# Attention scores and a graph layer's product as sums of three products of split fp32 operands

## The reference

```python
def _sparse_attention(x, src, dst, wq, bq, wk, bk, wv, bv, wo, bo):
    q = (x @ wq + bq).reshape(N, H, Dh) * Dh ** (-0.5)
    k = (x @ wk + bk).reshape(N, H, Dh)
    v = (x @ wv + bv).reshape(N, H, Dh)
    scores = jnp.einsum('ehd,ehd->eh', q[src], k[dst])
    ...
    out = jax.ops.segment_sum(attn[:, :, None] * v[dst], src, num_segments=N)
    return out.reshape(N, D) @ wo + bo
for i in range(NUM_BLOCKS):
    y = _cond_layer_norm(x, cond, s1_w[i], s1_b[i], b1_w[i], b1_b[i])
    x = x + _sparse_attention(y, src, dst, wq[i], ...)
    y = _cond_layer_norm(x, cond, s2_w[i], s2_b[i], b2_w[i], b2_b[i])
    x = x + jax.nn.relu(y @ m_w1[i] + m_b1[i]) @ m_w2[i] + m_b2[i]
...
out = jnp.zeros_like(x).at[col].add(x[row] * norm[:, None])
return out @ lin_w.T + lin_b
```

## Time and profile before

| | us |
|---|---|
| runs before, median of 3 (lowest to highest) | 1582.38 (1581.98 to 1583.31) |
| the profiled execution, its own time | 1580.26 |
| span of its profile | 1578.6 |
| TensorE busy | 1504.3 |
| VectorE busy | 1186.9 |
| ScalarE busy | 1076.5 |
| mean granted clock of TensorE | 0.99 |

### The profile page before, as it was taken

How to read it: one execution, slowest core, us unless ns; L and a number is a source line. 1 busy time by engine, 2 the same in 40 slices (tenths; PEclk the granted TensorE clock), 3 DMA queues, 4 the chain that set the end, 5 groups by cost and what they waited for, 6 DMA issues and landing times. The chain is left out here.

```text
span 1578.6 us, 26154 instructions
## 1 busy us (share of the span) xinstructions
PE 1504.3 (95%) x9086; PEld 1212.8 (77%) x9086; DVE 1186.9 (75%) x2055; ACT 1076.5 (68%) x1557; POOL 644.8 (41%) x468
## 2 busy tenths in 40 slices
PE   4999899999999999999999999999999999999987
PEld 4775687888788878887864688888888888888874
DVE  8998565656565656564733499999999999999967
ACT  8845455544564546454532389999999999999953
POOL 3541200120012001200301677888888888888501
PEclk9999899999999999999999999999999999999989
DMA  3002310122012201110204877777777777777600
GB/s 111 1 1 89 127 54 28 34 64 79 26 34 81 76 12 34 61 61 27 96 0 160 183 168 150 155 157 153 156 155 153 157 151 158 152 157 153 156 34 34
DMA packets 88590, 151.48 MB, mean 96 GB/s; under 512 B 23610, under 2 KB 28602, under 8 KB 88002
## 3 DMA queue, kind: packets, MB, share of 16 engines
q0 software_dynamic: 54400, 85.33, 27.7%
q1 hardware_dynamic: 34114, 65.15, 12.6%
HBM read 141.02 MB, written 9.31 MB: 95 GB/s over the span
## 5 line engine op out<-in xcount | busy, mean ns | idle before, releaser
L1911 POOL DMA_INDIRECT edge_gathered<-dst_table,edge_index x158 | 271.2, 1716 | 58.1 <-issue 36.9
L227 PE MATMUL edge_z2p<-edge_w_hi,edge_h_hi 128*128 128x512 f32 x628 | 252.2, 402 | 0.6 <-DVE edge_late L2278 0.6
L227 PE MATMUL edge_z2p<-edge_w_lo,edge_h_hi 128*128 128x512 f32 x628 | 248.0, 395 | 0.0
L1090 POOL TENSOR_TENSOR h<-h,tr_row_b 128x512 f32<-128x512 f32 x40 | 59.2, 1511 | 420.3 <-ACT C L1342 420.0
L1883 POOL DMA_INDIRECT edge_gathered<-src_table,edge_index x158 | 177.6, 1124 | 81.5 <-issue 79.3
L227 PEld LDWEIGHTS edge_z2p<-edge_w_hi,edge_h_hi 128*128 128x128 f32 x628 | 118.3, 188 | 32.3 <-issue 7.9
L227 PEld LDWEIGHTS edge_z2p<-edge_w_lo,edge_h_hi 128*128 128x128 f32 x628 | 118.4, 189 | 24.8
L227 PE MATMUL edge_z2p<-edge_w_hi,first_parts 128*128 128x512 f32 x316 | 125.4, 397 | 0.0
L1106 PE MATMUL tr_one<-tr_yT_hi,tr_w_hi 128*128 128x256 f32 (+2 forms) x384 | 121.3, 316 | 4.3 <-issue 4.3
L227 PE MATMUL edge_z2p<-edge_w_hi,edge_h_lo 128*128 128x512 f32 x312 | 123.3, 395 | 0.0
L1106 PE MATMUL tr_one<-tr_yT_hi,tr_w_lo 128*128 128x256 f32 (+2 forms) x384 | 118.6, 309 | 0.0
(11 more groups left out here) (390 smaller groups left out, 4013.5 us busy)
## 6 DMA issues: line engine op xcount, KB each, us to landing
w_c<-in_attr_T SPq DMA_DIRECT2D x78, 128.0 KB, 3.7
w_a<-in_wv SPq DMA_DIRECT2D x4, 1024.0 KB, 5.4
w_b<-in_wq SPq DMA_DIRECT2D x4, 1024.0 KB, 5.4
w_a<-in_wk SPq DMA_DIRECT2D x4, 1024.0 KB, 7.5
w_b<-in_wo SPq DMA_DIRECT2D x4, 1024.0 KB, 6.6
w_a<-in_m SPq DMA_DIRECT2D x4, 1024.0 KB, 5.1
w_b<-in_m SPq DMA_DIRECT2D x4, 1024.0 KB, 5.3
w_c<-in_cond_w SPq DMA_DIRECT2D x4, 768.0 KB, 5.4
```

The source lines that it names most:

```text
L227: mm = pe.matmul(out, a, b, start=(n == 0), stop=(n == last))
L1911: pool.indirect_dma_start(out=from_rows[ring][:, j, :].bitcast(F32), out_offset=None, in_=k.dst_table, in_offset=bass.IndirectOffsetOnAxis ...
```

## The change

The queries and keys become fp32r tensors with a remainder each. ScalarE now makes the rounded copy of queries and keys (the queries' scale is moved into the split of wq), and VectorE makes the remainder from the same bank (`rest_of`), which frees the bank. [...] No memory is added: the query remainders lie in `first_parts` and `hid_hi`, the key remainders in `w_lo[1]` and `hid_lo`. For that reason wo's low pieces move behind the first two heads (n=10 to 13), m1's to n=14 to 17, and the next block's first conditioning split to n=17 to 19. ScalarE's split of wo now stands behind the key copies, as its stream has one place for it. The perceptron's hidden copy moves from `qT` to `v`. In the graph layer, aggregate and lin_w are split in the same way, lin_w is loaded into `k.C` later than before, and its product is three fp32r matmuls for each chunk.

```diff
@@ -837,7 +837,7 @@
 FIRST, REST = slice(0, 3 * P), slice(3 * P, NP)
-PART_A = -(-NODES // 2)
+PART_A = 2 * (-(-NODES // 4))
 USED = 2 * PART_A
...
-        qT, kT, v = sb("qT", [P, KF, NP]), sb("kT", [P, KF, NP]), sb("v", [P, NT, D])
+        qT, kT, v = sb("qT", [P, KF, NP], F32R), sb("kT", [P, KF, NP], F32R), sb("v", [P, NT, D])
+        flat_first, flat_hid, flat_rest, flat_w = (t[:, :, :].rearrange("p a b -> p (a b)")
+                                                   for t in (k.first_parts, hid_hi, hid_lo, w_lo[1]))
+        q_lo = [[flat_first[:, i * P:(i + 1) * P] for i in range(NT)],
+                [flat_first[:, (NT + i) * P:(NT + i + 1) * P] for i in range(3)]
+                + [flat_hid[:, (2 * NT + i) * P:(2 * NT + i + 1) * P] for i in range(2)]] + [
+                [flat_hid[:, (a * NT + i) * P:(a * NT + i + 1) * P] for i in range(NT)] for a in range(2)]
+        k_lo = [flat_w[:, 0:USED], flat_w[:, USED:2 * USED], flat_rest[:, 0:USED], flat_rest[:, USED:2 * USED]]
...
-        hidden = qT
+        hidden = v[:, :, :].rearrange("p a b -> p (a b)").rearrange("p (c n) -> p c n", n=NP)
...
-        gcn_h, gcn_W, gcn_aggT = v, probsT[0], qT
-        gcn_wt = kT[:, :, :].rearrange("p c n -> p (c n)")[:, 0:KF * D].rearrange("p (c n) -> p c n", n=D)
+        gcn_h, gcn_W, gcn_wt = v, probsT[0], rows_of(k.C, KF)
...
-            for name, by in (("q", "sca"), ("k", "vec")):
+            for name, by in (("q", "low"), ("k", "low")):
...
-                plan.add(("agg", m, f), "sca", "two" if (m, f) in ((0, 0), (1, 0)) else "one")
+                plan.add(("agg", m, f), "low", "two" if (m, f) in ((0, 0), (1, 0)) else "one")
...
-                plan.need(sp, ("S", LAST, N - 1))
-                sp.dma_start(gcn_wt, k.dram["lin_w"].rearrange("(c p) n -> p c n", p=P)).then_inc(loaded["gcn_lin"], 16)
...
+                plan.need(sp, ("yT", LAST, 1, NT - 1))
+                sp.dma_start(gcn_wt, k.dram["lin_w"].rearrange("(c p) n -> p c n", p=P)).then_inc(loaded["gcn_lin"], 16)
...
+                    hi, last = qT[:, h, i * P:(i + 1) * P], LAST_ROWS if i == NT - 1 else P
                     for f in range(2):
-                        mm = pe.matmul(bank[:, f, 0:PART_A], qT[:, h, i * P:(i + 1) * P],
-                                       kT[:, h, f * PART_A:(f + 1) * PART_A], start=True, stop=True)
+                        at = slice(f * PART_A, (f + 1) * PART_A)
+                        out = bank[:, f, 0:PART_A]
+                        pe.matmul(out, hi, kT[:, h, at], start=True, stop=False)
+                        pe.matmul(out[0:last, :], q_lo[h][i][:, 0:last], kT[:, h, at], start=False, stop=False)
+                        mm = pe.matmul(out, hi, k_lo[h][:, at], start=False, stop=True)
...
-                pe.wait_ge(loaded["gcn_lin"], 32)
+                pe.wait_ge(w_split, of_weight("wv", BLOCKS) + PIECES)
...
-                    plan.made(chain(pe, bank[:, :], [(gcn_aggT[:, c, i * P:(i + 1) * P], gcn_wt[:, c, :]) for c in range(KF)]))
+                    plan.made(three(bank[:, :], node_pairs(of_tile(rows, i), "wv", range(KF))))
...
-                    act.activation(w_hi[a][:, :, :], w_raw[a][:, :, :], ACT.Copy).then_inc(w_high, PIECES)
+                    act.activation(w_hi[a][:, :, :], w_raw[a][:, :, :], ACT.Copy,
+                                   scale=DH ** -0.5 if name == "wq" else 1.0).then_inc(w_high, PIECES)
...
-                    for f in range(2):
-                        for m in range(KF):
-                            bank = plan.take(act, ("q", b, m, f))
-                            settle(k, act)
-                            at = QK_HALVES[f]
-                            n = at.stop - at.start
-                            plan.took(("q", b, m, f), act.activation(qT[:, m, at], bank[:, 0:n],
-                                                                     ACT.Identity, bias=bias_of(0, m), scale=DH ** -0.5))
-                            if f == 0:
-                                high_piece("wk", m)
+                    for which, name, dst in ((0, "q", qT), (1, "k", kT)):
+                        for f in range(2):
+                            for m in range(KF):
+                                bank = plan.take(act, (name, b, m, f))
+                                settle(k, act)
+                                at = QK_HALVES[f]
+                                n = at.stop - at.start
+                                act.activation(dst[:, m, at], bank[:, 0:n], ACT.Identity, bias=bias_of(which, m)
+                                               ).then_inc(o_high, 1)
+                                if (name, f) == ("q", 0):
+                                    high_piece("wk", m)
                     high("wo", b)
...
-                        if n == 10 and b < LAST:
+                        if n == 17 and b < LAST:
                             cut(b + 1, 0)
...
+                act.wait_ge(loaded["gcn_lin"], 32)
+                for c in range(PIECES):
+                    act.activation(w_hi[0][:, c, :], gcn_wt[:, c, :], ACT.Copy).then_inc(w_high, 1)
...
-                        plan.took(("agg", m, f), act.activation(gcn_aggT[:, m, f * HALF:(f + 1) * HALF], out, ACT.Copy))
+                        act.activation(yT_hi[:, m, f * HALF:(f + 1) * HALF], out, ACT.Copy).then_inc(y_high, 1)
...
-                    dve.tensor_tensor(w_lo[a][:, :, :], w_raw[a][:, :, :], w_hi[a][:, :, :].bitcast(F32),
-                                      ALU.subtract).then_inc(w_split, PIECES)
+                    if name == "wq":
+                        ins = dve.scalar_tensor_tensor(w_lo[a][:, :, :], w_raw[a][:, :, :], DH ** -0.5, w_hi[a][:, :, :].bitcast(F32),
+                                                       ALU.mult, ALU.subtract)
+                    else:
+                        ins = dve.tensor_tensor(w_lo[a][:, :, :], w_raw[a][:, :, :], w_hi[a][:, :, :].bitcast(F32), ALU.subtract)
+                    ins.then_inc(w_split, PIECES)
+                def rest_of(which, name, hi, b, m, f, pieces):
+
+                    dve.wait_ge(o_high, (3 * b + which) * (2 * HEADS) + (f * KF + m + 1))
+                    at = QK_HALVES[f]
+                    bank = plan.at[(name, b, m, f)].bank
+                    for out, lo, up in pieces:
+                        ins = dve.scalar_tensor_tensor(out, bank[:, lo - at.start:up - at.start], cb[:, b, which, m:m + 1],
+                                                       hi[:, m, lo:up].bitcast(F32), ALU.add, ALU.subtract)
+                    plan.took((name, b, m, f), ins)
...
-                    dve.wait_ge(o_high, b * (2 * HEADS) + (2 * h + f + 1))
+                    dve.wait_ge(o_high, (3 * b + 2) * (2 * HEADS) + (2 * h + f + 1))
...
-                own(dve.memset(qT[:, :, USED:NP], 0.0))
+                own(dve.tensor_scalar(qT[:, :, USED:NP], cols(k.ident[:, 0:KF * (NP - USED)], NP - USED), 0.0, None, ALU.mult))
...
-                    low("wk", b)
                     for f in range(2):
-                        at = QK_HALVES[f]
-                        n = at.stop - at.start
                         for m in range(KF):
-                            bank = plan.take(dve, ("k", b, m, f))
-                            plan.took(("k", b, m, f), dve.tensor_scalar(kT[:, m, at], bank[:, 0:n],
-                                                                        cb[:, b, 1, m:m + 1], None, ALU.add))
-                            if f == 0 and m >= 1:
-                                low_piece("wo", b, m - 1)
-                            if (f, m) == (1, 0):
-                                low_piece("wo", b, KF - 1)
+                            query_rest(b, m, f)
+                            if f == 0:
+                                low_piece("wk", b, m)
+                    for f in range(2):
+                        for m in range(KF):
+                            key_rest(b, m, f)
...
-                        if 5 <= n < 5 + PIECES:
-                            low_piece("m1", b, n - 5)
-                        if n in (12, 13) and b < LAST:
-                            cond_low(b + 1, n - 12)
+                        if 10 <= n < 10 + PIECES:
+                            low_piece("wo", b, n - 10)
+                        if 14 <= n < 14 + PIECES:
+                            low_piece("m1", b, n - 14)
+                        if n in (18, 19) and b < LAST:
+                            cond_low(b + 1, n - 18)
...
+                    if i < PIECES:
+                        dve.wait_ge(w_high, of_weight("wv", BLOCKS) + i + 1)
+                        dve.tensor_tensor(w_lo[0][:, i, :], gcn_wt[:, i, :], w_hi[0][:, i, :].bitcast(F32),
+                                          ALU.subtract).then_inc(w_split, 1)
...
+                for f in range(2):
+                    for m in range(KF):
+                        half, bank = slice(f * HALF, (f + 1) * HALF), plan.at[("agg", m, f)].bank
```

(18 more changed lines are left out.)

## The result

| | before | after |
|---|---|---|
| median of 16 runs each, us | 1582.47 | 1588.06 (1583.04 to 1590.09) |
| ratio of after to before, 95% interval | | 1.0032 (1.0024 to 1.0039) |
| the profiled execution, us | 1580.26 | 1589.95 |
| TensorE busy, us | 1504.3 | 1499.9 |

A forecast was written before the change was run, and what follows sets the result against it. TensorE, busy 95% of the span, was taken to decide alone in attention steps 8 to 19. Scores +4.8, clock +5.2, halves +0.6, graph layer -3.4 make +7.2 us; with the median 2.1 above the profiled execution, 1589.6 us, range 1579 to 1597.

The forecast's parts named there:

- The gap: Attention start, each block: TensorE idle 3.6 us before transposing row 0's probabilities, waiting for ScalarE's late exponential and VectorE's scaling.
- Late at T(7): Attention loop, each block: the transposes of row 7's probabilities still come 2.7 us late after partial catching up.
- The clock: Behind the idle time, TensorE's clock falls to the 1.2 GHz level: +1.3 us a block, +5.2.
- the third rival: Clock stays low until row 7's transposes: +4.7 to 5 us a block, 1609 us; chance 0.08.
- The rival in which it holds: Clock holds through TensorE's idle time before row 0's transposes, or recovers within it: +2.0, 1584.4 us; chance 0.22.
- The tile: Attention scores: a tile takes 0.89 us as six fp32r matmuls of 314 columns, against 1.06 before.
- Steps 10 to 19: Later attention steps: smaller score tiles give back 1.7 us a block, less 0.5 charged for waits where half heads end.
- S(0) and S(1): The first two score tiles, made in the key phase, save 0.35 us a block.
- The graph layer: Linear product as fp32r matmuls: each of five tiles saves 0.68 us, -3.4 us in all.
- Hidden, 0.24 us of cover at the narrowest: Query projections: ScalarE's copy and VectorE's remainder free each bank about 1.2 us behind its product, costing nothing.
- Wider halves, +0.6: Projections and attended products: column halves of 314 and 372 add a little TensorE work, +0.6 us.
- The rival "all kept": Exponentials not late, each of 80 score tiles gives its 0.17 us: -16.4, 1566 us; chance 0.12.

The follow-up runs named there:

- run 5: Kernel before, fp32 scores, with only the change's ScalarE order (wo split between last key product and row 0's exponential) and later VectorE weight subtractions: 1594.97 us, ratio 1.0080.
- run 1: Changed kernel with ScalarE's wo split moved from before row 0's exponential into four pieces in steps 4 to 7, m1's to 8 to 11: 1573.95 us, ratio 0.9959.
- run 4: Changed kernel with 18 useless matmuls issued by TensorE before its wait for the first probability transposes, results overwritten: 1583.08 us, ratio 1.0009 to the kernel before.
- run 2: Changed kernel with the exponential of row 0 moved ahead of ScalarE's last key copy: 1576.0 us, ratio 0.9959 to the kernel before.
- run 3: Changed kernel with both edits: wo split in pieces in later steps, and row 0's exponential ahead of the last key copy: 1568.38 us, ratio 0.9915.
- run 6: Kernel before with only the graph layer's linear product changed to three products of split parts: 1577.87 us, ratio 0.9973.
- run 10: Changed kernel with only ScalarE's wait for wk moved behind the second query copy, wk's pieces one half tile later: 1583.71 us, ratio 1.0015.

## Why the prediction was right, and where it was off

**The gap.** Forecast 3.6 us before T(0) by a sum of key copy, split, exponential and scaling; measured 3.31 in all blocks. Run 5 shows that the order on ScalarE makes most of it (2.73 us) without any of the new products, run 1 that the split's 1.9 us is over half of it.

**Late at T(7).** Forecast 2.7 us; measured 2.4 at full clock (run 4).

**The clock.** Forecast 1.3 us a block, 5.2 in all; measured 0.90 to 1.82, 5.6 in all, by run 4 against the changed kernel. That it came so close is partly luck. The clock doesn't fall behind every such gap, and over all runs it cost less: run 4 against the changed kernel is 3.6 us by the ratios, 5.0 by the medians. The working behind the 1.3 us doesn't hold either: it has S(3) and two sets of transposes at 1.0 us, where the tile's 0.89 and the transposes' 0.55 of the third rival give 2.0. T(0) to T(1) took 2.67 us in three of the blocks with the low clock and 1.92 in run 4. The clock is also the likeliest reason for the spread: the changed kernel's runs with a mean granted clock of 0.989 took 1583.0 to 1584.2 us, those with 0.983 took 1589.4 to 1590.1. The rival in which it holds, 1584.4 us, is what the fastest runs show.

**The other rule on the clock.** By the Trainium skill, TensorE: Matmul & The Clock Gate, Part 4: PE-mode transpose, transposes would not help it to rise, which was the rival of 1609 us. In the changed kernel the window from 390 to 394 us, with its transposes, is at 1.00. Matmuls run among them, so the rule itself is neither borne out nor refuted; its consequence here didn't come.

**The tile.** Forecast 0.89 us; measured 0.87 (S(2)'s start to T(0)'s in runs 2 and 3, six matmuls 0.145 apart) against 1.06. The Trainium skill, FP8 and Floating Point Precision, TensorE Precision Notes, counts four passes for true fp32, from which 0.80 us was the estimate for three; the measured tiles are in the ratio of 0.82 and not 0.75. Steps 10 to 19 gave 1.0 to 1.4 us a block net of the half heads' chain, forecast 1.2. S(0) and S(1) gave 0.34 in three blocks and 0.20 in block 0, forecast 0.35.

**The graph layer.** Forecast -3.4; measured -3.37 (and -3.33 alone, run 6).

**The steps that failed.** "Hidden, 0.24 us of cover at the narrowest", for the query banks, was wrong in two ways. I looked at the copy's length and not at what the copy waits for: the load of wk. Before, one release by ScalarE was just in time; with VectorE's remainder behind it the third product is late by up to 0.37 us, and the first four products by 0.6 in two blocks. The load landed up to 0.3 us later behind the first product than before, too, but in run 5, with the old queries, such a load cost only 0.1 us (8.28 in block 1). And the narrow halves cost 0.30 us a block in run 10 too. There the bank's own cycle of copy and remainder is longer than the 1.44 us of a narrow product. The last wide query of block 1 (its last matmul starts at 360.61 and the next product at 360.78), and the matmul that needs its bank:

```profile
361.06 0.57 ACT L1395 ACTIVATE tr_qT<-tr_one,tr_cb 128x372 fp32r<-128x372 f32 x1 [0.95 <-PE tr_one L1112]
361.67 0.60 DVE L1533 SCALAR_TENSOR_TENSOR tr_hid_hi<-tr_one,tr_cb,tr_qT 128x372 fp32r<-128x372 f32 x1 [0.83 <-ACT tr_qT L1395]
362.33 0.38 PE L1112 MATMUL tr_one<-tr_yT_hi,tr_w_hi 128*128 128x256 f32 x1
```

The bank is free 1.5 us behind its product, not 1.2. Together, 0.6 + 0.6 and 3 x 0.3, that is 2.1 us in blocks 1 to 3 of the profiled execution, where the sum had nil. The other way, "Wider halves, +0.6" did not show: four query products of 372 columns take the 8.16 us that four of 370 took, and the keys' first four take 0.15 less in each block. Why the keys became faster was not tested.

**The sum.** In the profiled executions the terms measure 3.6 for the scores (forecast 4.8), 5.6 for the clock (5.2), -0.6 for the halves (0.6), 2.1 for the queries (nil) and -3.4 for the graph layer (-3.4). That is 7.3 against 7.2, but misses of 1.2, 1.2 and 2.1 us cancel in it. So the number's nearness is partly luck, while the gap, the lateness and the graph layer came from the mechanism. The forecast also took the median to lie 2.1 us above the profiled execution; in the changed kernel it lies 1.9 below.

**The size of the saving.** The rival "all kept" gave 1566 us, and run 3, with T(0) 0.87 us behind S(2) in every block, comes near at 1568.4. But all of it is not kept: its tiles give 9.5 us (1.2 in S(0) and S(1), 3.5 until T(7), 4.8 behind it) where 80 tiles smaller by 0.19 would give 15. The rival's point of decision, T(0) within 0.2 us of S(2)'s end, is not enough either: run 2 meets it in every block and takes 1576, since its gap comes before T(1).

## What to carry to other kernels

When work is moved from one engine to another, list what stands behind it there in program order: with ScalarE's order mended the same change is worth 13 us (run 3), and one weight split of 1.9 us and one key copy ahead of the first exponential, with the waits and the clock behind them, cost nearly 20. Order alone, and no arithmetic, turned +0.3% into -0.9%. A wait for a load that cost little ahead of a loop becomes dear once a second engine must follow the first before a bank comes free.

## What the runs showed that was not expected

- The same gap does not always bring the clock down. Behind 3.31 us of idleness (3.59 in one block) it fell in seven of eight blocks (the changed kernel and run 10), behind 2.73 us in three of four (run 5), behind 1.90 in two of four (run 2), behind 1.51 in none of four (run 1), and behind 0.62 following 18 matmuls in none of four (run 4). What decides it for one and the same gap these runs don't show. The changed kernel, with such gaps, spreads over 7 us in 16 runs; run 3, without them, over 3 us in five.
- Useless matmuls in a gap paid: run 4 does 2.6 us of them per block and its ratio to the kernel before is 1.0009, where the changed kernel has 1.0032: 3.6 us for four times 2.6 us of work.
